# A fused macaron block on one core: the attention's scores from fp32 queries and keys

## The reference, cut to what matters

```
x = x + 0.5 * ffn(layernorm(x))
x = x + attention(layernorm(x))
x = x + 0.5 * ffn(layernorm(x))
```

```
q = (x @ Wq.T + bq);  k = (x @ Wk.T + bk);  v = (x @ Wv.T + bv)
scores = q . k / sqrt(16)
scores = where((j <= i) & (j > i - 32), scores, FP16_MIN)
m = max(scores.max(-1), sink_bias);  e = exp(scores - m)
out = (e / (e.sum(-1) + exp(sink_bias - m))) @ v
```

## Time and profile before

| | |
|---|---|
| median of 3 runs | 375.26 us (374.29 to 377.11) |
| the profiled execution, its own time | 374.08 us |
| its span, first to last instruction | 372.3 us |
| TensorE busy (weight loads) | 314.2 us, 84% (269.3 us) |
| ScalarE, GpSimd, VectorE busy | 240.8, 203.9, 170.5 us |
| chain that ended last | TensorE 52%, GpSimd 13%, VectorE 11%, ScalarE 6%, transfers 6% |

### The profile page before, as it was taken

The page is one execution under the profiler, slowest core; times in us unless marked ns, Lnnn a source line. Parts: engine busy times, 40 slices in busy tenths (PEclk is TensorE's granted clock), DMA queues, the critical chain, the costliest instruction groups (busy, mean ns, idle before and its releaser), DMA issues.

```text
span 372.3 us, 10763 instructions
## 1 busy us (share of the span) xinstructions
PE 314.2 (84%) x3591; PEld 269.3 (72%) x3599; DVE 170.5 (46%) x623; ACT 240.8 (65%) x666; POOL 203.9 (55%) x220
## 2 busy tenths in 40 slices
PE   0692999999736998999895789999999699979991
PEld 0372988989636867899775588899888488868881
DVE  6997248400026479464782658826457330000005
ACT  4971577778624968959531787995974268847640
POOL 5206677777774875124417775745442577776500
PEclk9996799999976899999996999999999989989998
DMA  7793755555263244101136233324223745553131
GB/s 233 233 240 94 258 175 169 153 195 184 79 197 128 96 161 106 66 37 57 61 128 223 97 102 125 103 85 136 89 65 107 261 139 193 194 141 104 37 121 56
DMA packets 39222, 50.51 MB, mean 136 GB/s; under 512 B 5803, under 2 KB 23296, under 8 KB 39170
## 3 DMA queue, kind: packets, MB, share of 16 engines
q1 hardware_dynamic: 33192, 37.73, 29.5%
q0 software_dynamic: 5888, 12.07, 12.5%
q10 hardware_dynamic: 90, 0.03, 0.0%
HBM read 16.32 MB, written 9.18 MB: 68 GB/s over the span
## 4 chain that ended last, share of the span: by engine, by line
PE 52%; POOL 13%; issue 11%; DVE 11%; ACT 6%; DMA 6%; SPq 1%; DVEq 0%; ACTq 0%
PE y L619 16%; POOL xg L498 7%; PE z L583 5%; POOL yd L506 5%; PE y L634 4%; PE z L585 4%; PE z L584 4%; PE m L801 3%; PE y L622 3%; DVE x L1212 2%; DMA xg<-xr,from_row 2%; PE m L680 2%; PE m L654 2%; ACT h L877 2%; PE m L789 2%
## 5 line engine op out<-in xcount | busy, mean ns | idle before, releaser
L877 ACT ACTIVATE h<-z,w_tile 128x128 f32<-128x128 f32 x368 | 105.2, 373 | 40.0 <-PE z L585 37.6
L506 POOL DMA_INDIRECT yd<-ysb,to_row x92 | 91.7, 997 | 58.0 <-ACT ysb L890 38.6
L498 POOL DMA_INDIRECT xg<-xr,from_row x92 | 91.4, 993 | 58.6 <-issue 40.8
L619 PE MATMUL y<-w,h 128*128 x736 | 105.2, 288 | 0.0
L619 PEld LDWEIGHTS y<-w,h 128*128 128x128 f32 x736 | 93.0, 197 | 1.4
L583 PE MATMUL z<-xgt,w_tile 128*128 128x128 f16 x368 | 71.0, 229 | 12.1 <-ACT xgt L934 5.6
L584 PE MATMUL z<-xgt,w_tile 128*128 128x128 f16 x368 | 70.6, 227 | 0.0
L585 PE MATMUL z<-xgt,w_tile 128*128 128x128 f16 x368 | 70.6, 227 | 0.0
L583 PEld LDWEIGHTS z<-xgt,w_tile 128*128 128x128 f16 x368 | 37.2, 101 | 19.5 <-issue 8.6
L934 ACT ACTIVATE xgt<-m 128x512 f16<-128x512 f16 (+1 forms) x48 | 27.1, 590 | 25.0 <-PE m L680 24.8
L1112 DVE SCALAR_TENSOR_TENSOR x<-y,x 128x512 f32<-128x512 f32 x8 | 5.5, 690 | 79.7 <-PE y L639 79.7
(11 more groups left out here) (197 smaller groups left out, 468.1 us busy)
## 6 DMA issues: line engine op xcount, KB each, us to landing
w_tile<-w SPq DMA_DIRECT2D x92, 258.0 KB
stage<-yd SPq DMA_DIRECT2D x8, 512.0 KB, 4.4
stage<-in_L_ffn_W_dram SPq DMA_DIRECT2D x8, 256.0 KB, 6.2
xr<-xs SPq DMA_DIRECT2D x8, 256.0 KB, 2.6
w<-in_L_ffn_W_dram SPq DMA_DIRECT2D x8, 256.0 KB, 4.8
xg<-xr,from_row POOLq DMA_INDIRECT x92, 2.7
yd<-ysb,to_row POOLq DMA_INDIRECT x92, 2.6
x<-in_L_attn_x_dram SPq DMA_DIRECT2D x4, 256.0 KB, 4.4
```

The costliest lines, as they stand in the source:

```text
L498: pool.indirect_dma_start(out=xg[:, r % XR, :], out_offset=None, in_=xr[ph], in_offset=bass.IndirectOffsetOnAxis(ap=from_row[:, ph, i:i + ...
L506: pool.indirect_dma_start(out=yd[ph], out_offset=bass.IndirectOffsetOnAxis(ap=to_row[:, ph, i:i + 1], axis=0), in_=ysb[:, r % YR, :], in_o ...
L619: pe.matmul(to, h32[:, u % HB, c * P:(c + 1) * P], w2[:, bass.ds(e, 1), c, :].rearrange("p a d -> p (a d)"), start=(c == 0), stop=False, s ...
L877: op = act.activation(h32[:, u % HB, cols], z[:, u % 2, cols], ACT.Gelu, bias=bias[:, c:c + 1], scale=1 / WS)
```

## The change

- `qm` is fp32 and there are two of it, one for even sequences (in the memory of `stage`) and one for odd ones (`qm1`).
- The masked queries are made by VectorE in one step, straight from the bank of `qk`: 4 instructions (one for each head), each a multiplication with `head_scale` and an addition of `head_bias`, which hold the scale and the bias where the head's rows are and 0 elsewhere. They are made once from `head` and `bq`. They give the bank free and raise `q_ready`. The step is called `q_masked` in place of `split`; it waits for the scores of the sequence two before.
- ScalarE only reads the keys, into an fp32 buffer of the layout that `k_hi` and `k_lo` had (`keys`, in place of `qk32` and `qkhi`).
- A strip and head group of the scores is one fp32 matmul in place of three fp16 ones. The scores also wait until the keys have been read.
- In VectorE's table `q_masked` of sequence 1 stands at 42.55 (`split` stood at 43.14) and that of sequence 3 at 68.0 (69.56); each is now ahead of the first `smax` of the sequence before (42.62 and 68.08).

```diff
-    ('att_lo', 2): 64.2, ('att_stats', 3): 64.35, ('att_shift', 3): 64.98, ('vals', 2): 65.13, ('split', 2): 66.02,
-    ('att_lo', 3): 67.22, ('smax', 2, 0): 68.08, ('split', 3): 69.56, ('smax', 2, 1): 70.66, ('vals', 3): 72.1,
+    ('att_lo', 2): 64.2, ('att_stats', 3): 64.35, ('att_shift', 3): 64.98, ('vals', 2): 65.13, ('q_masked', 2): 66.02,
+    ('att_lo', 3): 67.22, ('smax', 2, 0): 68.08, ('q_masked', 3): 68.0, ('smax', 2, 1): 70.66, ('vals', 3): 72.1,
...
-        qm = stage[:, HT * 2 * D:HT * 2 * D + BT * HG].bitcast(F16)\
-            .rearrange("p (k s h q) -> p k s h q", k=2, h=HG, q=WIN)
+        qm = [stage[:, HT * 2 * D:HT * 2 * D + BT * HG].rearrange("p (s h q) -> p s h q", h=HG, q=WIN),
+              sb("qm1", [P, STRIPS, HG, WIN])]
...
                 pe.wait_ge(q_ready, b + 1)
+                moved(pe, USE[("qk", b)] + 1)
...
-                        op = three(bank(k + g)[:, i * KW:(i + 1) * KW],
-                                   qm[r, 0, s, :, :].rearrange("p h q -> p (h q)"),
-                                   qm[r, 1, s, :, :].rearrange("p h q -> p (h q)"),
-                                   k_hi[r, b % 2, s * WIN:s * WIN + KW], k_lo[r, b % 2, s * WIN:s * WIN + KW],
-                                   start=False)
+                        op = pe.matmul(bank(k + g)[:, i * KW:(i + 1) * KW], qm[b % 2][r, s, :, :].rearrange("p h q -> p (h q)"),
+                                       k32[r, b % 2, s * WIN:s * WIN + KW], start=False, stop=True,
+                                       skip_group_check=True)
...
-            def queries_keys32(b):
...
+            def keys(b):
+                k = USE[("qk", b)] + 1
                 act.wait_ge(m_ready, k + 1)
                 if b >= 2:
                     act.wait_ge(m_ready, USE[("scores", b - 2, 1)] + 2)
-                act.activation(q_hi[:, :], q32[:, :], ACT.Copy).then_inc(q_hi_done, 1)
-                act.activation(k_hi[:, b % 2, WIN:], k32[:, :], ACT.Copy).then_inc(q_hi_done, 1)
+                act.activation(k32[:, b % 2, WIN:], bank(k), ACT.Identity, bias=bk[:, :], scale=1 / WS)\
+                    .then_inc(m_done[k % MB], 1)
...
+            def mask_queries(b):
+
+                k = USE[("qk", b)]
+                dve.wait_ge(m_ready, k + 1)
+                dve.wait_ge(masks_made, 8)
+                if b >= 2:
+                    dve.wait_ge(m_ready, USE[("scores", b - 2, 1)] + 2)
+                for h in range(HG):
+                    op = dve.tensor_scalar(qm[b % 2][:, :, h, :], bank(k).rearrange("p (s q) -> p s q", q=WIN),
+                                           head_scale[:, h:h + 1], head_bias[:, h:h + 1], ALU.mult, ALU.add)
+                op.then_inc(m_done[k % MB], 1)
+                moved(dve, k)
+                dve.sem_inc(q_ready, 1)
...
+                dve.wait_ge(aw_loaded, 16 * AW_LOADS)
+                dve.tensor_scalar(head_scale[:, :], head[:, :], 0.25 / WS, None, ALU.mult)
+                dve.tensor_scalar(head_bias[:, :], head[:, :], bq[:, 0:1], 0.25, ALU.mult, ALU.mult).then_inc(masks_made, 1)
...
-                    dve.memset(k_hi[:, s, 0:WIN], 0.0)
-                    dve.memset(k_lo[:, s, 0:WIN], 0.0)
+                    dve.memset(k32[:, s, 0:WIN], 0.0)
```

More of the change, by code:

```diff
@@ L101 @@
     ('xevict', 1, 4): 35.51, ('xevict', 1, 5): 36.51, ('att_xn', 0): 36.52, ('att_hi', 0): 37.01,
-    ('att_xn', 1): 37.02, ('qk32', 0): 38.01, ('qkhi', 0): 38.51, ('att_hi', 1): 38.52, ('xevict', 1, 6): 40.01,
-    ('qk32', 1): 42.01, ('qkhi', 1): 42.02, ('xevict', 1, 7): 44.51, ('exp', 0): 44.52, ('pt32', 0, 0): 46.01,
+    ('att_xn', 1): 37.02, ('keys', 0): 38.01, ('att_hi', 1): 38.52, ('xevict', 1, 6): 40.01,
+    ('keys', 1): 42.01, ('xevict', 1, 7): 44.51, ('exp', 0): 44.52, ('pt32', 0, 0): 46.01,
     ('exp', 1): 46.51, ('pt32', 0, 1): 46.52, ('xevict', 1, 8): 46.53, ('xevict', 1, 9): 46.54, ('pt32', 1, 0): 46.55,
@@ L106 @@
     ('tanh', 2): 54.51, ('xevict', 2, 0): 61.01, ('att_xn', 2): 62.01, ('att_hi', 2): 63.01, ('xevict', 2, 1): 63.02,
-    ('xevict', 2, 2): 63.03, ('qk32', 2): 64.51, ('xevict', 2, 3): 64.52, ('qkhi', 2): 64.53, ('att_xn', 3): 64.54,
-    ('att_hi', 3): 65.51, ('xevict', 2, 4): 67.01, ('xevict', 2, 5): 67.02, ('qk32', 3): 68.01, ('qkhi', 3): 68.51,
+    ('xevict', 2, 2): 63.03, ('keys', 2): 64.51, ('xevict', 2, 3): 64.52, ('att_xn', 3): 64.54,
+    ('att_hi', 3): 65.51, ('xevict', 2, 4): 67.01, ('xevict', 2, 5): 67.02, ('keys', 3): 68.01,
     ('xevict', 2, 6): 69.01, ('exp', 2): 71.51, ('pt32', 2, 0): 73.01, ('exp', 3): 73.51, ('pt32', 2, 1): 73.52,
@@ L121 @@
     ('masks',): 20.5, ('comb', 0, 0): 33.93, ('comb', 0, 1): 34.73, ('att_stats', 0): 35.75, ('att_stats', 1): 36.47,
-    ('att_shift', 0): 37.24, ('att_shift', 1): 38.35, ('att_lo', 0): 38.98, ('split', 0): 40.61, ('att_lo', 1): 42,
-    ('vals', 0): 42.1, ('smax', 0, 0): 42.62, ('split', 1): 43.14, ('smax', 0, 1): 44.26, ('vals', 1): 45.13,
+    ('att_shift', 0): 37.24, ('att_shift', 1): 38.35, ('att_lo', 0): 38.98, ('q_masked', 0): 40.61, ('att_lo', 1): 42,
+    ('vals', 0): 42.1, ('smax', 0, 0): 42.62, ('q_masked', 1): 42.55, ('smax', 0, 1): 44.26, ('vals', 1): 45.13,
     ('smax', 1, 0): 45.53, ('smax', 1, 1): 46.03, ('pv_norm', 0, 0): 46.35, ('pv_norm', 0, 1): 46.77,
@@ L272, in macaron_kernel @@
         aw_hi, aw_lo = sb("aw_hi", [P, AW], F16), sb("aw_lo", [P, AW], F16)
-        bq, bq4, bk = sb("bq", [P, 1]), sb("bq4", [P, 1]), sb("bk", [P, 1])
+        bq, bk = sb("bq", [P, 1]), sb("bk", [P, 1])
         bv, bo, sink = sb("bv", [P, KVD]), sb("bo", [P, D]), sb("sink", [P, 1])
-        head = sb("head", [P, HG])
+        head, head_scale, head_bias = sb("head", [P, HG]), sb("head_scale", [P, HG]), sb("head_bias", [P, HG])
         near, late, win = sb("near", [P, KW]), sb("late", [P, KW]), sb("win", [P, HS + 1, KW], BF16)
@@ L323, in macaron_kernel @@
         comb_step, combined = sem("comb_step"), sem("combined")
-        xa_hi_done, q_hi_done, q_split, q_ready = sem("xa_hi_done"), sem("q_hi_done"), sem("q_split"), sem("q_ready")
+        xa_hi_done, q_ready = sem("xa_hi_done"), sem("q_ready")
         v_ready, mx_done, mxs_done = sem("v_ready"), sem("mx_done"), sem("mxs_done")
@@ L1004, in extras @@
                         attended_hi(*arg)
[L1005 to L1008, removed]
+                    if name == "keys":
+                        keys(*arg)
                     if name == "exp":
@@ L1408, in extras @@
                         attended_lo(*arg)
-                    if name == "split":
-                        split_masked(*arg)
+                    if name == "q_masked":
+                        mask_queries(*arg)
                     if name == "vals":
```

21 lines of the change are left out of this document (2 added, 19 removed).

## The result

The changed kernel takes 392.49 us (median of 4 runs, 391.95 to 393.5), the kernel before 376.19 us in the runs beside it (4 runs, 374.29 to 377.43). The ratio is 1.0435, with a 95% interval of 1.0401 to 1.0468. The profiled execution took 393.5 us with a span of 391.7; it is the longest of its four, and the one of before (374.08 us) is the shortest of its own, so the profiles lie 19.4 us apart where the medians lie 16.3 apart. I take amounts from the medians and places from the profiles. A ratio leaves out an execution that lies over 1.5% above the fastest of its kernel, so it need not be the quotient of the medians.

A forecast was written before the change was run, and what follows sets the result against it. TensorE's order beside the attention was taken to set the end. 8.4 - 1.1 + 2.9 = 10.2 us on the profiled 374.08 gives 384.3, or 385.5 us as median; forecast's own range 382 to 389, whole range 379 to 400.

The forecast's parts named there:

- Side-by-side fp32 loads (8.4 us): Scores on TensorE: loads of both row halves run in parallel, 1.05 us more a half, 8.4 us for 8 halves.
- The two rivals on its price: Scores: fp32 loads one after another, 2.81 us more a half, chance 0.20; a cheap product, 0.24 more, chance 0.12.
- loads one after another: Scores: the two row halves' fp32 loads do not overlap, 22.5 us more in all, 399.5 us; chance 0.20.
- Taken back (1.1 us): Earlier TensorE waits beside the attention that the change removes or covers: 0.3, 0.3, 0.2 and 0.33 us, 1.1 in all.
- The four pieces: TensorE's waits: `xa_lo` of sequence 1 0.3 us, banks for `pv` 0.3, scores (1, 0) 0.2, `xgt` behind scores (2, 0) 0.33.
- The split by sequences: Time lost: about 3.4 us beside sequences 0 and 1, 6.8 us beside 2 and 3, including the 2.9 us wait.
- The new wait (2.9 us): TensorE ahead of scores (2, 1) waits 2.9 us, since `q_masked` of sequence 3 delays `smax` (2, 0) on VectorE.
- 3 x 0.61 + 0.68 = 2.5 us: VectorE: four `q_masked` instructions of sequence 3, three at 0.61 us apart and a last of 0.68, together 2.5 us.
- The cost of the wait: The wait ahead of scores (2, 1) enters the sum at its own length, 2.9 us, with nothing added for the clock.
- 3 us more than my forecast: Clock loss behind the wait at scores (2, 1): 3 us of work at half speed, 388.5 us; no separate chance.
- In sequence 0 the same swap costs nothing: VectorE, sequence 0: `q_masked` of sequence 1 ahead of `smax` (0, 0) costs nothing; scores (0, 1) use other banks.
- Faster than before, VectorE's line: Attention from queries' product to `q_ready`: VectorE sets the end, so a gain of 4.0 us, 371.3 us; chance 0.05.

The follow-up runs named there:

- The first experiment: The changed kernel with `q_masked` of sequence 3 back behind `smax` (2, 0) on VectorE (69.56 for 68.0): 383.63 us, ratio 1.0202.
- the filled one: The changed kernel with 16 unread fp16 matmuls on TensorE where it waits ahead of scores (2, 1): 387.15 us, ratio 1.0283.
- the cheapest product with no wait: The changed kernel with queries and keys in fp16, low parts left out, and `q_masked` of sequence 3 behind `smax` (2, 0): 377.13 us, ratio 0.9996.

## Why the prediction was right in kind, and 7 us short

- **Side-by-side fp32 loads (8.4 us): right.** Forecast 1.05 us more for a half, measured 1.12, or 9.0 us for 8 halves. The two rivals on its price, 2.81 and 0.24 us more, fall: with the row halves apart the half takes 3.32 us. The absolute figure was a little low (1.76 against 1.93 us): 16 pairs at 0.112 us make 1.78, and the start and the end of the group take 0.15 more. The old half had 0.10 of the like (0.71 forecast, 0.81 measured), so most of it drops out of the difference. The time alone would not have told: 392.5 us lies midway between my 385.5 and the 399.5 of loads one after another.
- **Taken back (1.1 us): near, and the sum by some luck.** The first experiment has the whole change without the new wait: 7.4 us by the medians, forecast 8.4 - 1.1 = 7.3. It holds 9.0 us of scores, so 1.6 and not 1.1 were not paid, and two small misses cancel. The four pieces were not tried one by one. The split by sequences did not come out: in the profiles of that experiment and of before, 5.8 us are lost by the router behind sequences 0 and 1 (188.6 against 182.8) where I said 3.4, and 4.7 behind 2 and 3 where 3.9 stood without the wait. These profiles lie 10.3 us apart where the medians lie 7.4 apart, so the places are rough. A part of the first is a stretch at half the clock at 163 us that the profile of before does not have. Why it is there I have not found; it is in the changed kernel, in the first experiment and in the filled one.
- **The new wait (2.9 us): right in place and cause, under-sized.** It is 3.66 us. The step that was short is "3 x 0.61 + 0.68 = 2.5 us" for `q_masked`: from its start to the next instruction's it takes 3.11 us, with 0.72 from one instruction's start to the next and 0.80 for the last (2.97 us for four), instead of 0.61 and 0.68. `smax` behind it has the 2.88 us foreseen.
- **The cost of the wait: the step that failed.** The sum has the wait at its own length and leaves the clock to a rival, "3 us more than my forecast", which it counts in the forecast's own range, 382 to 389; the measured time lies 3.5 us above that. The filled wait shows 5.3 us: 3.0 right behind it, as that rival had it, and the rest in later stretches. This is the largest part of the miss. 385.5 + 0.6 for the halves - 0.5 for what was not paid + 0.8 for the wait + 5.3 for the clock + 0.9 for the median of before (376.2 in these runs, not 375.3) is 392.6, and 392.49 was measured. The terms are from single profiles and medians with some 1 us of spread, so that the sum closes this well is luck too.
- **"In sequence 0 the same swap costs nothing": right, and more than that.** No wait for VectorE stands there in the changed kernel. And the swap is needed there, since the queries' bank is now emptied by VectorE; I had named other banks as the reason and missed that one.
- **Faster than before, VectorE's line:** falls. Even the cheapest product with no wait is at 0.9996.

## What to carry to other kernels

A wait of TensorE in a stretch that is otherwise full has two prices, its length and the lower clock behind it, and the second can be the larger: here 3.7 and 5.3 us. So before an instruction is moved ahead of the work that frees a bank, look at who waits for that bank; and when the emptying of a bank passes from one engine to another, each place in the order has to be looked at again, since the place that one sequence needs can be the one that harms the next. Small fp32 products in different row halves must alternate in the order, or they cost 1.7 times as much and the clock besides.

## What the runs showed of the hardware

- Fp32 products of 64 rows and 64 columns run in pairs at 0.112 us for each pair of records when the row halves alternate, and at the same 0.112 for a single record when they do not (0.104 on average over a half, since some records overlap where the two groups meet).
- The granted clock fell to its lower level (0.62 over 136 to 140 us) right behind a half of unpaired fp32 products, with TensorE busy 15.95 of the 16 us from 128 to 144 us. With the row halves alternating it was 1.00 there. So a busy engine did not keep its clock. It was seen in this one kernel, and why is open.
- Matmuls whose result nobody reads keep the clock up (0.50 to 1.00 over 239.0 to 245.8 us) and pay where TensorE's order sets the end behind them; in front of transfers they brought nothing.
- VectorE's scaling and biasing of 512 fp32 columns from PSUM takes 0.72 us from one instruction to the next, where a reduction over as many takes 0.61.
